# Two attention stages of a graph network: the last chunk's scores and chain of maxima in one piece behind the chunk ahead of it

## The reference, cut to what matters

```python
# layer 2
logits = leaky_relu(a_s[src] + a_d[dst], 0.2)        # self loops are appended to src and dst
m = segment_max(logits, dst)
e = exp(logits - m[dst])
den = segment_sum(e, dst)
out = segment_sum(e / (den[dst] + 1e-16) * h[src], dst)
# layer 3: logits = leaky_relu(a_src[src] + a_dst[dst] + a_edge, 0.2), the rest alike, without loops
```

## Time and profile before

| | |
|---|---|
| median of 3 runs | 3252.54 us (3248.59 to 3256.95) |
| the profiled execution | 3248.09 us, with a span of 3246.0 us |
| PE busy | 2527.9 us, 78% of the span |
| DVE busy | 2300.0 us, 71% |
| ACT busy | 1696.6 us, 52% |
| POOL busy | 1516.6 us, 47% |
| attention stage of layer 2, first scores to last add | 1850.2 to 2424.9 us |
| attention stage of layer 3, first scores to last add | 2588.2 to 3160.4 us |

### The profile page before, as it was taken

The page is one execution under the profiler, slowest core; times in us unless marked ns, Lnnn a source line. Parts: engine busy times, 40 slices in busy tenths (PEclk is TensorE's granted clock), DMA queues, the critical chain, the costliest instruction groups (busy, mean ns, idle before and its releaser), DMA issues. The chain is left out here.

```text
span 3246.0 us, 56122 instructions
## 1 busy us (share of the span) xinstructions
PE 2527.9 (78%) x12612; PEld 1928.6 (59%) x12613; DVE 2300.0 (71%) x5860; ACT 1696.6 (52%) x4048; POOL 1516.6 (47%) x1759
## 2 busy tenths in 40 slices
PE   2999998596999999999984488887860577878870
PEld 1888887444666666666663366666650455666650
DVE  4788887574788788778775367676778466766767
ACT  1666665322555555555552466666641466666651
POOL 1333333103444555455440377777730377777740
PEclk9999999798999999999996678778875777878885
DMA  2100000225556666565640355555522455555521
GB/s 68 24 10 8 10 9 9 60 67 177 152 159 166 161 164 165 153 168 159 164 122 24 113 134 139 137 139 137 139 60 35 116 142 142 142 142 141 142 64 39
DMA packets 186874, 349.20 MB, mean 108 GB/s; under 512 B 74641, under 2 KB 117034, under 8 KB 186507
## 3 DMA queue, kind: packets, MB, share of 16 engines
q0 software_dynamic: 83520, 249.39, 30.4%
q1 hardware_dynamic: 103239, 98.62, 10.5%
HBM read 325.45 MB, written 22.44 MB: 107 GB/s over the span
## 5 line engine op out<-in xcount | busy, mean ns | idle before, releaser
L1759 POOL DMA_INDIRECT t_rows<-table_h,t_istage x896 | 854.6, 954 | 266.0 <-issue 248.6
L1846 PE MATMUL t_pso<-t_rows,t_hot 125*125 125x272 f32 (+1 forms) x1792 | 597.3, 489 | 104.6 <-DVE t_rows L1885 64.3
L1335 POOL DMA_INDIRECT b_rows<-table_kv,b_istage x448 | 458.8, 1024 | 378.5 <-PE b_pso L1471 252.9
L1846 PEld LDWEIGHTS t_pso<-t_rows,t_hot 125*125 125x125 f32 x1792 | 402.7, 236 | 202.5 <-issue 105.5
L1397 ACT COPY b_asked<-b_psq 125x512 f32<-125x512 f32 x224 | 131.1, 585 | 427.6 <-PE b_psq L1436 427.6
L1885 DVE TENSOR_TENSOR t_rows<-t_rows,t_psm 125x1056 f32<-125x1056 f32 x224 | 276.7, 1235 | 63.5 <-issue 63.4
L1832 PE MATMUL t_pss<-node_scores,t_hot_t 125*125 x1792 | 266.2, 279 | 33.7 <-ACT t_hot_t L1790 31.1
L1832 PEld LDWEIGHTS t_pss<-node_scores,t_hot_t 125*125 125x125 f32 x1792 | 260.5, 225 | 49.1 <-issue 44.1
L1797 ACT ACTIVATE t_hot<-con_iota,g_dstl 125x125 f32<-125x125 f32 x896 | 280.3, 384 | 0.0
L1895 DVE TENSOR_TENSOR acc<-acc,t_pso 125x272 f32 (+1 forms) x448 | 192.7, 430 | 118.2 <-DVE acc L1895 69.1
L1436 PE MATMUL b_psq<-queries,b_hot_t 125*125 x896 | 235.6, 386 | 45.4 <-issue 23.7
(11 more groups left out here) (394 smaller groups left out, 4961.5 us busy)
## 6 DMA issues: line engine op xcount, KB each, us to landing
t_places<-targets SPq DMA_DIRECT2D x56, 488.3 KB
t_rows<-table_h,t_istage POOLq DMA_INDIRECT x896, 3.7
b_attr<-in_attr_t SPq DMA_DIRECT2D x224, 62.5 KB
b_places<-targets SPq DMA_DIRECT2D x28, 488.3 KB
b_rows<-table_kv,b_istage POOLq DMA_INDIRECT x448, 5.4
table_h<-d_stage SPq DMA_DIRECT2D x50, 132.8 KB
t_flag<-flags SPq DMA_DIRECT2D x56, 62.5 KB
table_kv<-d_moved SPq DMA_DIRECT2D x25, 128.9 KB
```

The source lines that it names most:

```text
L1335: pool.indirect_dma_start(out=rows[:, h, s, :], out_offset=None, in_=table, in_offset=bass.IndirectOffsetOnAxis(ap=istage[:, h, s:s + 1], ...
L1759: pool.indirect_dma_start(out=rows[:, r, s, :], out_offset=None, in_=table, in_offset=bass.IndirectOffsetOnAxis(ap=istage[:, r, s:s + 1], ...
L1846: mm = pe.matmul(ps_o[b % 2][0:P, at:at + mw], hot[:, r, b * G + u, :], rows[0:P, r, b * G + u, 0:mw], start=u % PAIR == 0, stop=u % PAIR ...
```

## The change

The flag `chain` now ends one chunk earlier: `body(26)` holds no dealt-out part of the chain on any engine. In its place a closing part stands behind the whole of `body(26)`: DVE adds the last block of chunk 26, works out the scores of chunk 27 (`rate`, which `body(25)` no longer does), and then goes through the whole chain (`link` for steps 0 to 2, then `tie`); PE runs its four `link` steps behind all sums of chunk 26; ACT runs `wane` and `weigh` behind all its one-hot tiles of chunk 26. In `body(27)` the add of chunk 26's last block falls away, as it has been done. All other chunks keep the order they had; the operations are the same in number and shape. The moved code became functions; their bodies are those of the lines removed, cut here with "...".

```diff
@@ -1800,22 +1800,31 @@
+                def wane(c):
+                    act.wait_ge(fading, c + 2)
+                    act.activation(fade[:, 1], fade[:, 0], ACT.Exp).then_inc(faded, 1)
+
+                def weigh(c):
+                    act.wait_ge(gapped, c + 2)
+                    act.activation(weight, gap[:, 0], ACT.Exp).then_inc(weighed, 1)
+                    if own:
+                        act.activation(loopw[:], gap[:, 1], ACT.Exp).then_inc(weighed, 1)
+
                 def body(c, r, i):
-                    chain = not known(c, -1) and not ends_at(c, CHUNKS - 1)
+                    chain = not known(c, -1) and not ends_at(c, CHUNKS - 2)
                     for b in range(B):
                         ahead, hence = (block_at(c, r, i, b + k) for k in (LEAD + 1, 2))
                         if b == 2 and chain:
-                            act.wait_ge(fading, c + 2)
-                            act.activation(fade[:, 1], fade[:, 0], ACT.Exp).then_inc(faded, 1)
+                            wane(c)
                         if ahead:
                             turn(*ahead)
                         if b == 3 and chain:
-                            act.wait_ge(gapped, c + 2)
-                            act.activation(weight, gap[:, 0], ACT.Exp).then_inc(weighed, 1)
-                            if own:
-                                act.activation(loopw[:], gap[:, 1], ACT.Exp).then_inc(weighed, 1)
+                            weigh(c)
                         if hence:
                             spot(*hence)
+                    if ends_at(c, CHUNKS - 2) and not ends_at(c, CHUNKS - 1):
+                        wane(c)
+                        weigh(c)
                 act.wait_ge(setup, 2)
                 turn(0, 0, 0, 0)
                 spans(act, body)
...
+                def link(c, r, b):
+                    if b == 0:
+                        pe.wait_ge(scored, c + 2)
+                        pe.transpose(peak_t, peak[:].rearrange("p s h -> p (s h)"), ident[0:P, 0:P]).then_inc(turned, 1)
...
+                    if b == 3:
+                        pe.wait_ge(hotset, (c + 1) * B + 1)
+                        pe.wait_ge(peaked, c + 2)
+                        pe.matmul(factor, hot[0:1, (r + 1) % RING, 0, :], fade[:, 2], start=True, stop=True)
+                        pe.transpose(most_e, most[:], ident[:]).then_inc(returned, 1)
+
                 def body(c, r, i):
-                    chain = not known(c, -1) and not ends_at(c, CHUNKS - 1)
+                    chain = not known(c, -1) and not ends_at(c, CHUNKS - 2)
                     fresh = not ends_at(c, CHUNKS - 2)
...
+                        if chain:
+                            link(c, r, b)
                         if fresh:
                             expand(*later(c, r, i, 2), b, word)
                         if not known(c, 0):
                             total(c, r, i, b)
+                    if ends_at(c, CHUNKS - 2) and not ends_at(c, CHUNKS - 1):
+                        for b in range(B):
+                            link(c, r, b)
                 pe.wait_ge(setup, 2)
@@ -1916,16 +1932,58 @@
+                def tie(c, e):
+                    dve.wait_ge(returned, e + 1)
+                    steps = most_e.rearrange("p (s h) -> p s h", h=H)
+                    if own:
+                        dve.tensor_tensor(gap[:, 1], loop[:], steps, ALU.subtract)
+                    dve.tensor_tensor(gap[:, 0], score[:], steps, ALU.subtract).then_inc(gapped, 1)
+                    if not known(e, 1):
+                        dve.wait_ge(rescaled, e)
+                    dve.tensor_copy(held[:], factor).then_inc(holding, 1)
+
+                def link(e, h, j, b, k):
+                    opens, closes = flag[:, h, 0], flag[:, h, 1]
+                    if b == 0:
+                        dve.wait_ge(turned, e + 1)
+                        dve.wait_ge(laned[h], j * 32 + 32)
+                        dve.tensor_tensor_scan(head[:], opens, peak_t, -BIG, ALU.add, ALU.max)
+                        dve.tensor_tensor_scan(tail[:, ::-1], closes, peak_t[:, ::-1], -BIG, ALU.add, ALU.max).then_inc(scanned, 1)
...
+                    if b == 2:
+                        dve.wait_ge(colled, e + 1)
+                        k.then(dve.tensor_copy(init[:], starts))
+                        k.then(dve.tensor_tensor_scan(run[:], opens, peak_t, init[:, 0:1], ALU.add, ALU.max))
+                        dve.wait_ge(faded, e + 1)
+                        dve.tensor_scalar(fade[:, 2], fade[:, 1], -1.0, None, ALU.add).then_inc(factored, 1)
+                        dve.wait_ge(factored, e + 1)
+                        dve.tensor_tensor_scan(most[:, ::-1], closes, run[:, ::-1], init[:, 1:2], ALU.add, ALU.max).then_inc(peaked, 1)
                 def body(c, r, i):
-                    chain = not known(c, -1) and not ends_at(c, CHUNKS - 1)
+                    chain = not known(c, -1) and not ends_at(c, CHUNKS - 2)
+                    closing = ends_at(c, CHUNKS - 2) and not ends_at(c, CHUNKS - 1)
                     e, h, j = later(c, r, i, 1)
                     k = Tally(dve, dv, e * STEPS_OF + BEGUN)
                     k.n = 3 if own else 2
-                    opens, closes = flag[:, h, 0], flag[:, h, 1]
                     past = None if known(c, 1) else load_stairs(dve, g, c - 1)
                     now = None if known(c, 0) else load_stairs(dve, g, c)
                     for b in range(B):
-                        last = block_at(c, r, i, b - 1)
+                        last = None if b == 0 and ends_at(c, CHUNKS - 1) else block_at(c, r, i, b - 1)
...
                         if chain and b == 3:
+                            tie(c, e)
                         if last:
                             add(*last, past if b == 0 else now)
...
+                        if chain and b < 3:
+                            link(e, h, j, b, k)
+                    if closing:
+                        add(c, r, i, B - 1, now)
+                        assert rate(e, h, j) == (3 if own else 2)
+                        for b in range(3):
+                            link(e, h, j, b, k)
+                        tie(c, e)
+                    elif not ends_at(c, CHUNKS - 3):
                         assert rate(*later(c, r, i, 2)) == (3 if own else 2)
-                    if chain:
+                    if chain or closing:
                         assert k.n == STEPS_OF, k.n
```

More of the change, by code:

```diff
@@ L1854, in body @@
                     for b in range(B):
-                        if chain and b == 0:
-                            pe.wait_ge(scored, c + 2)
-                            pe.transpose(peak_t, peak[:].rearrange("p s h -> p (s h)"), ident[0:P, 0:P]).then_inc(turned, 1)
-                        if chain and b == 1:
-                            pe.wait_ge(scanned, c + 2)
-                            pe.transpose(ends_row[:, 0:128], head[:, P - 1:P], ident[:])
-                            pe.transpose(ends_row[:, 128:256], tail[:, 0:1], ident[:]).then_inc(rowed, 1)
-                        if chain and b == 2:
-                            pe.wait_ge(begun, c + 2)
-                            pe.matmul(starts[:, 0:1], begins[:, 0].rearrange("a s h -> a (s h)"), unit[:], start=True, stop=True)
-                            pe.matmul(starts[:, 1:2], begins[:, 1].rearrange("a s h -> a (s h)"), unit[:], start=True, stop=True).then_inc(colled, 1)
-                        if chain and b == 3:
-                            pe.wait_ge(hotset, (c + 1) * B + 1)
-                            pe.wait_ge(peaked, c + 2)
-                            pe.matmul(factor, hot[0:1, (r + 1) % RING, 0, :], fade[:, 2], start=True, stop=True)
-                            pe.transpose(most_e, most[:], ident[:]).then_inc(returned, 1)
+                        if chain:
+                            link(c, r, b)
                         if fresh:
@@ L1936, in body @@
                         if chain and b == 3:
-                            dve.wait_ge(returned, e + 1)
-                            steps = most_e.rearrange("p (s h) -> p s h", h=H)
-                            if own:
-                                dve.tensor_tensor(gap[:, 1], loop[:], steps, ALU.subtract)
-                            dve.tensor_tensor(gap[:, 0], score[:], steps, ALU.subtract).then_inc(gapped, 1)
-                            if not known(e, 1):
-                                dve.wait_ge(rescaled, e)
-                            dve.tensor_copy(held[:], factor).then_inc(holding, 1)
+                            tie(c, e)
                         if last:
@@ L1973, in body @@
-                        if chain and b == 2:
-                            dve.wait_ge(colled, e + 1)
-                            k.then(dve.tensor_copy(init[:], starts))
-                            k.then(dve.tensor_tensor_scan(run[:], opens, peak_t, init[:, 0:1], ALU.add, ALU.max))
-                            dve.wait_ge(faded, e + 1)
```

(3 more changed lines are left out.)

46 lines of the change are left out of this document (24 added, 22 removed).

## The result

The changed kernel takes 3260.98 us, the median of 16 runs (3256.22 to 3269.15); the kernel before, in 16 runs beside them, 3249.77 (3244.33 to 3256.95). The ratio is 1.0038 with a 95% interval of 1.003 to 1.0045: slower by 0.38%, or some 12 us (the two medians differ by 11.2). The profiled execution took 3258.88 us, its span 3257.1.

The account below looks back on a forecast made before the run. No engine bound by its mean (TensorE 78%, DVE 71%); DVE's last add ends each stage. Terms gave 38.5 against 33.0 and 38.1 against 34.6: +9.0 on 3252.54, so 3261.5 us, range 3255.1 to 3264.9 (chance 0.73).

Parts of the forecast that it names:

- (a): DVE's step from an add straight into chunk 26, at the end of each stage: 1.3 us.
- (b): Chunk 26 without the chain but with its own last add: 13.35 us in both layers.
- (c): On DVE, from chunk 26's last add to chunk 27's scores, where no gather is late: 0.42 us.
- (d): Chunk 27's scores on DVE, same work but later: 1.14 us, with one operation fewer in layer 3.
- (e): The chain of maxima alone behind chunk 26: 7.7 us, from 6.7 to 8.1; with (d), 0.4 less in layer 3.
- (f): The step into chunk 27, with ACT's exponentials fitting within it: 1.0 us.
- (g): Chunk 27 without chunk 26's last add, PE's first sum slow: 13.6 us in both layers, bounds 11.9 to 14.6.
- Nothing outside the two stretches changes: Claim that only the ends of layer 2's and layer 3's stages change, so +9.0 us is added to the median.
- the high bound: Both stage ends with the largest terms: 40.2 and 39.8 us, +7.2 and +5.2, +12.4 in all.
- Late gathers: Rival, last scores: longer gather waits get hidden; a gain needs over 6.2 us in layer 2, 6.95 in layer 3; chance 0.12.
- The clock low over all of chunk 27: Rival: four slow PE sums make chunk 27 17.5 us instead of 13.6; +16.8 us in all, 3269; chance 0.12.
- The change separates nothing: Rival: queues run ahead, so chain and messages still overlap; excluded for DVE, only the 13.35 could shorten; no own chance.

Follow-up runs that it names:

- the kernel with fillers: Changed kernel plus 27 unread matmuls on PE ahead of and behind the chain's parts; 3610.42 us, ratio 1.0052 to the kernel before.
- the one-layer kernels: New order in one layer only, against the kernel before: layer 2 alone 3609.35 us, ratio 1.0041; layer 3 alone 3599.86 us, ratio 1.0011.
- the one with the block dealt out: Against the changed kernel, scores follow chunk 26's first message and chain parts are spread among later ones; 3253.3 us, ratio 1.0001 to the kernel before.
- the second four experiments: Changed kernel again 3262.82 us; last gathers delayed in old order 3265.38, in new order 3260.11; chain spread within chunk 26 3253.3; kernel before 3250.8.

## Why the prediction was right, and where it wasn't

The forecast was 3261.5, and 3260.98 was measured. Some of that closeness is luck: the forecast was +9.0 on a median of 3252.54, and the measurement is +11.2 on one of 3249.77. The mechanism was right: hops laid bare, a slow first sum behind them, and little waiting freed in return. Step by step, first value layer 2, second layer 3:

- (a) The step into chunk 26: 1.3 forecast; 1.29 and 1.29.
- (b) Chunk 26 with its own last add: 13.35 forecast; 13.65 and 12.69. These are the two values of the earlier trace rows, 13.67 and 13.05, the second a little shorter; the mean for both was 0.3 too low and 0.66 too high, and the errors cancel in part.
- (c) Add to scores: 0.42 forecast; 0.04 and 0.04. The 0.42 of the earlier trace rows is a mean over the stages, most of it from the loop. In code that is written out there is next to nothing between add and scores in the old order too: 0.03 to 0.04 where no gather was late.
- (d) The scores: 1.14 and some 0.86 forecast; 1.14 and 0.94.
- (e) The bare chain: 7.7 forecast, a little less in layer 3; 7.86 and 7.45. Taking the chain of chunk 0 and subtracting the two delays that belong to other work was the step that carried the prediction: it gave 8.1, and a further 0.4 was taken off for two hops at 2.4 GHz. The result held within 0.2, but only the first hop met that clock; the second did not (0.50, and 0.63 us where the kernel with fillers has 0.41).
- (f) The step into chunk 27: 1.0 forecast; 0.71 and 0.91, ended by ACT's exponentials and not by registers.
- (g) Chunk 27: 13.6 forecast; 14.26 and 13.97. Mis-sized by 0.66 and 0.37: the sixteen matmuls took 6.19 in layer 2, 0.6 more than the 5.59 of the earlier trace rows, and 5.46 in layer 3, which before had eight in 2.02.

The sums are 38.95 and 37.29, forecast 38.5 and 38.1; together the ends grew by 8.63, forecast 9.0. The step that failed is the sentence "Nothing outside the two stretches changes". Layer 3's steady part grew by 6.1 us in the pair of profiles behind the result, and by 12.0 on the chip where no wait for a gather hid it. The rest of the difference between the two spans (11.1 = 8.63 + 6.1 in layer 3's steady part - 3.6 elsewhere) has the size of what single executions scatter. As I set the chance of "within 0.3%" at 0.51 and of "slower by over 0.3%" at 0.45, the measured 0.38% fell on the side that I took for a little less likely. The ends alone would be 0.27%, so the extra outside them is what tips it over the 0.3%, as far as single profiles can say.

Three readings in the prediction were off, without effect on the forecast. The terms of the high bound add up to 40.3 and 39.9, not 40.2 and 39.8, so that it is +12.6. The chain's price inside chunk 26, "only 1.6 to 2.2 more", was read against a chunk with five adds, where chunk 26 of before has four. With the same nine adds in both kernels, chunks 26 and 27 without their steps took 15.22 + 13.67 = 28.89 us (layer 2) and 14.88 + 13.05 = 27.93 (layer 3) before, and 13.65 + 14.26 = 27.91 and 12.69 + 13.97 = 26.66 after. So the chain dealt out cost 1.0 and 1.3 us, and somewhat more if the slower first sum of the kernel after is taken off (its 16 matmuls took 0.6 and 1.4 us longer). And PE did not stand "nearly idle" ahead of both slow stretches of the earlier trace rows: from 2389.0 to 2396.2 it was busy for 4.19 of 7.20 us, and its gaps right ahead of the slow sums were 2.16 and 2.24 us.

The rivals. Late gathers: not here (0.70 and 3.45 in the old order, as in the earlier trace rows); with late gathers made on purpose, the ends favour the new order by 6.8 us where 6.3 was worked out; no run had a wait near the point of no return, and the totals don't settle the sign. The clock low over all of chunk 27: no, the sums that follow the first sixteen matmuls are fast in both layers (2.07 and 2.02 for eight), and the windows show 0.99 from 2418 on. But at four of the fourteen stage ends with a bare chain and no fillers (over all profiles), 24 matmuls took 8.7 to 8.9 us and not 16 some 5.5, so a part of this rival does occur. The Trainium skill, page "TensorE: Matmul & The Clock Gate", Part 1, has the throttled state as the default and activity as what releases it; the runs agree from both sides, with 0.50 after the bare chain and 1.00 where unused matmuls filled it. "The change separates nothing" was excluded, and rightly.

What stays open is why layer 3's loop loses time when layer 2's last chunks are written otherwise. The traces show where on DVE (the loop's return, at most 7.3 before and 9.2 after; an add just behind it; the copy into `begins`), and the one-layer kernels show that it isn't layer 3's own order. That the place of the loop's code in DVE's program matters is a reading that fits, but it isn't shown: the kernel before executes 56122 instructions, the changed one 56116, the ones with one layer changed 56119, the one with the block dealt out 56120, all engines taken together, so that the code behind layer 2's end may well lie elsewhere. PE's lower clock in the same stretch may follow from DVE's waits or lengthen them; no run tells these apart. In the loop of layer 3 instructions are fetched all the time, as often before as after; the queue's row in the view of DMA queues (packets, MB, share of the 16 engines) over that stretch is the same in both:

```profile
q14 instruction: 40, 0.33, 0.2%
```

The Trainium skill, page "Runtime: NRT & Kernel Launch", section "Instruction fetch mechanics", says that instructions are fetched ahead in blocks, in order only, and that a jump to a block that isn't loaded stalls the engine. By that rule the loop's return pays, and what it pays depends on where the block boundaries fall in the loop. The 7.3 us at the return and its growth to 9.2 agree with it, as does a stall that comes back at the same instruction in each round. Two things it doesn't explain by itself: one of the eight marks stands in chunk 1, ahead of the loop, and layer 2's loop returns in at most 1.8 us in both kernels on the first chip. And no run moved the code alone. The kernel before with a few instructions that do nothing ahead of layer 3 would tell.

## What to carry to other kernels

A chain that goes back and forth between engines costs its hops only when nothing else stands between its parts: here the same operations added 1.0 to 1.3 us dealt out among messages (a little more at an equal clock) and 7.5 to 7.9 in one piece. Before a block is moved to hide one wait, count the hops that its new place lays open, and the slow first work of an engine that idled meanwhile; the wait has to be longer than both (here 6 to 7 us by the ends, and it was 0.70 and 3.45). And to price a bare chain, look for the one place where the kernel already runs it without company, usually the start of a stage, and subtract what was in its way there.

## What the runs showed of the hardware that I had not expected

- Code that a change doesn't touch can get slower: 6 to 12 us in layer 3's stage. A wait of DVE for itself (0.47 us) stands at one instruction in each of the loop's seven rounds and once ahead of it, the long waits at the loop's six returns grew by 6.5 us in all, and PE's granted clock over the stage fell from 0.79 to 0.76. The cause is open.
- The same kernel takes 3250 us on the chips of the result and of the second four experiments, and 3593 and 3607 on two others, and much of the difference lies in the looped stages (layer 3's steady part: 538 us against 663 and 659 in the kernel before). DVE is busy there for the same 388 to 390 us on both, so the difference is waiting. Why the chips differ, no run shows. Where it takes 3593 and 3607, no gather wait was left ahead of the last scores, so a change that hides such waits is worth less there.
- Unused matmuls kept PE's clock up (1.00 in place of 0.50, 3.83 us for 6.19), but gave nothing that the total shows: 1.9 us at the two ends together, and the first hop of the chain doubled with them.
